# Mamba-style fusion kernel on one core: the second half of z goes through another PSUM bank and is copied to SBUF before its SiLU

## Chip, core and metric

The kernel runs on one core of a Trainium2 chip. The metric is the time of one execution on the device in microseconds (us). The version before the change takes 1730.51 us (median of three executions, 1729.14 to 1731.21).

## What is computed

64 sequences of 114 tokens (a class token, 36 image patches, 77 text tokens), width 256. After a layer norm comes a selective state-space block, then a gated feed-forward with a small mixture of experts. All is fp32. What matters here is the state-space block (D_INNER 512, 16 states):

```python
xz = x @ W_in
xi, z = jnp.split(xz, 2, axis=-1)
xc = silu(depthwise causal conv of xi, 4 taps, + conv_b)
dt, Bm, Cm = jnp.split(xc @ W_x, ...)
delta = softplus(dt @ W_dt + b_dt)
dA = exp(delta * A);  dBu = delta * Bm * xc
h = dA_t * h + dBu_t;  y_t = h . C_t          # scan over the tokens
y = ys + xc * D
return y * silu(z) @ W_out
```

## The kernel before

Sequences are taken two at a time: 32 groups of 2 x 114 = 228 columns. The code calls a group's turn a step `i`. Within step `i` the scan of group `i` is cut into 16 units `k`, each a [128 x 912] tile. For each unit:

- POOL (GpSimd) multiplies u by B into the SBUF ring `xr` (`dbu`, L1646);
- ACT (ScalarE) writes exp(delta * A) into one of two PSUM slots (`exps`, four instructions, L1010);
- DVE (VectorE) scans (L1307);
- the product with C is made by DVE (L1316) for ten units, and by POOL (L1654) for the six units listed in `ON_POOL`;
- PE (TensorE) adds the states up into bank YB (`reduce_states`, L711), with a D-term in front of every fourth unit (L708), which at units 0 and 8 waits until DVE has read the bank (`y_out`, L1324).

The other stages are hung on the units by hand, `if k == 7 and runs(i + 2)` and so on: the order on each engine is the order of these lines, and semaphores tie the engines together. Group `i+2` gets its tokens (L625 at k=0), centring (L635), variance (L642), x projection (L610) and convolution (L661). Group `i+1` gets B, C and dt (L685 at k=1), delta (L697), softplus (L1058 to L1066), and z (L610 at k=13). Groups `i-1`, `i-2`, `i-3` get the output projection, the second norm and the feed-forward: `ffn_in` L756, `ffn_sigmoid` L1102 to L1106, `v_center` L767 at k=0, its square L1110, `v_var` L771, `ln3_rstd` L1115 and L1117, `v_norm` L1390.

SiLU needs another activation table than exp and ln. So after the exps of unit 1 ACT has a "window": load the table, SiLU of x (four instructions, L1041), SiLU of z in two halves (L1047), load the first table back (L1132). The exps of unit 2 come behind it.

PSUM has eight banks: four for the two slots, YB, and AB, BB, CB, which all side stages share. Before the change z's first half is in AB, its second half in CB. CB also holds the convolution of x, so the second half of z cannot be projected before the window has taken x out of CB (`pe.wait_ge(xs_done, 2 * g + 3)` in `proj_z`). DVE's `y_out` at k=1 multiplies the last units' sum of the step before by silu(z).

The copy `dbl_copy` (L1052, ACT, ahead of the exps of unit 5) waits for L685. On ACT the exps of unit 5 and `ln3_rstd` stand behind it, and DVE's `v_norm` (after unit 4) waits for `ln3_rstd`; the scan of unit 5 stands behind `v_norm`.

Of the kernel before, what the change touches and what calls it, by code (L numbers as in the profile page):

```python
# [15 lines left out]
ON_POOL = (1, 3, 8, 10, 12, 14)  # L16


def fusion_kernel(nc, x_patches, txt_t, tok_w, tok_b, cls_t, pos_t, w_in, conv_w, conv_b, w_x, w_dt, b_dt,
# [42 lines left out]
    with ExitStack() as whole:  # L62
# [20 lines left out]
        with ExitStack() as ctx:  # L83
# [149 lines left out]
            def ffn_free(e, g):  # L233

                if g == GROUPS - 2:
                    e.wait_ge(var_mm, GROUPS)
                elif g == GROUPS - 1:
                    e.wait_ge(z_mm, 2 * GROUPS)
# [28 lines left out]
            def z_bank(half):  # L267
                return pair((AB, CB)[half])
# [76 lines left out]
            z_mm = sem("z_mm")  # L345
            sz_done = sem("sz_done")
            dbl_mm = sem("dbl_mm")
# [95 lines left out]
            with nc.Block() as block:  # L443
# [161 lines left out]
                def _(pe):  # L605
# [8 lines left out]
                    def bank_c(g):  # L614

                        need(pe, xs_done, 2 * g)
                        need(pe, sz_done, 2 * (g - 1))
# [27 lines left out]
                    def proj_x(g, p, half):  # L645
                        if half == 0:
                            pe.wait_ge(xh_done, g + 1)
                        elif runs(g - 4):

                            pe.wait_ge(x2t_ev, g - 3)  # L650
                        else:
                            need(pe, delta_done, 2 * g)
                        project(p, x_bank(half), 2 * half * P).then_inc(xi_mm, 1)
# [11 lines left out]
                    def proj_z(g, p, half):  # L665

                        if half == 1 and runs(g + 1):
                            pe.wait_ge(xs_done, 2 * g + 3)
                        elif half == 1:
                            pe.wait_ge(sz_done, 2 * g)  # L670

                        elif runs(g - 3):
                            pe.wait_ge(v_done, g - 2)
                        elif runs(g - 2):
                            pe.wait_ge(h2_ev, g - 1)
                        else:
                            pe.wait_ge(delta_done, 2 * g + 1)
                        project(p, z_bank(half), (CH + 2 * half) * P).then_inc(z_mm, 1)
# [9 lines left out]
                    def proj_delta(g):  # L688
                        pe.wait_ge(dbl_ev, g + 1)

                        if runs(g - 4):
                            pe.wait_ge(o_done, g - 3)
                        else:
                            need(pe, sz_done, 2 * g - 1)
                        for half in range(2):
                            for c in range(2):
                                mm = pe.matmul(dt_bank(half)[:, c], wdt[32:33 + R, (2 * half + c) * P:(2 * half + c + 1) * P],  # L697
                                               dbl[32:33 + R, :], start=True, stop=True)
                            mm.then_inc(dt_mm, 1)
# [34 lines left out]
                    def h2_turn(g):  # L734
                        pe.wait_ge(h2n_done, g + 1)

                        if runs(g + 3):
                            pe.wait_ge(delta_done, 2 * g + 8)
                        else:
                            pe.wait_ge(x2t_ev, g)  # L740
                        for k in range(DC):
                            for s in range(SEQ):
                                mm = pe.transpose(x2t_ps[:, k, s], h2n[0:T, s, k * P:(k + 1) * P], ident[0:T, 0:T])
                        mm.then_inc(x2t_mm, 1)
# [15 lines left out]
                    def v_center(g):  # L760

                        pe.wait_ge(v_done, g + 1)
                        if runs(g + 3):
                            pe.wait_ge(sz_done, 2 * g + 7)
                        elif g == GROUPS - 3:
                            pe.wait_ge(h2_ev, GROUPS)
# [19 lines left out]
                    def bias_rows():  # L786
# [3 lines left out]
                        pe.wait_ge(sz_done, 2 * GROUPS)  # L790
# [4 lines left out]
                    def before_first():  # L795
# [5 lines left out]
                        var(1)  # L801
                        for half in range(2):
# [3 lines left out]
                        for half in range(2):  # L806
                            proj_z(0, 0, half)
# [9 lines left out]
                    def body(i):  # L817
# [5 lines left out]
                        for k in range(UNITS):  # L823
# [26 lines left out]
                            if k == 13 and runs(i + 1):  # L850
                                proj_z(i + 1, 1 - p, 1)
# [6 lines left out]
                            if k == 7 and runs(i + 2):  # L858
# [135 lines left out]
                def _(act):  # L994
# [19 lines left out]
                    def center_out(g, p):  # L1014
                        act.wait_ge(cent_mm, g + 1)
                        need(act, z_mm, 2 * g - 2)
# [27 lines left out]
                    def z_silu(g, p, half):  # L1044
                        act.wait_ge(z_mm, 2 * g + 1 + half)
                        need(act, y_done, CH // 2 * (g - 2) + half + 1)
                        nc.scalar.activation(sz[:, p, 2 * half:2 * half + 2], z_bank(half), ACT.Silu).then_inc(sz_done, 1)  # L1047
# [76 lines left out]
                    def window(i, p):  # L1124
# [4 lines left out]
                        if runs(i):  # L1129
                            z_silu(i, p, 0)  # L1130
                            z_silu(i, p, 1)
# [4 lines left out]
                    def before_first():  # L1136
# [7 lines left out]
                        rstd_out(1)  # L1144
                        x_out(1, 0)
# [11 lines left out]
                    def body(i):  # L1157
# [5 lines left out]
                        for k in range(UNITS):  # L1163
# [20 lines left out]
                            if k == 12 and runs(i - 1):  # L1184
# [8 lines left out]
                            if k == 4 and runs(i + 1):  # L1193
                                dbl_copy(i + 1)
                            if k == 12 and runs(i + 2):
# [612 lines left out]
```

## Time and profile before

| | |
|---|---|
| median of three executions | 1730.51 us |
| the profiled execution | 1728.77 us, its span 1726.7 us |
| one step in the steady stretch (u at 727.66 and 776.92 us on POOL) | 49.26 us |
| granted clock of TensorE, mean of the span | 0.947 of full speed |

Busy time says how long an engine had an instruction running. Three engines are busy for nine tenths of the span, so the time is read from which of them waits for which in one step, and not from the busy shares. The steady stretch runs from some 200 us to 1540 us. Step 16 is the one that the rows show: its unit 0 is scanned from 800.41 us, its window on ACT runs from 800.61 to 806.44 us. PEclk in a row is the granted clock as a share of 2.4 GHz: 1.00 is 2.4 GHz, 0.50 is 1.2 GHz, values between are means of the two.

### The profile page before, as it was taken

The numbers are of one execution on the slowest core, as the hardware profiler recorded it, in microseconds if no ns is written. First come the engines' busy times: TensorE is split into PE (matmuls) and PEld (weight loads), VectorE is DVE, ScalarE is ACT, GpSimd is POOL, SyncE is SP. The second block draws the span as 40 slices with busy tenths as digits, with TensorE's granted clock in tenths as the row PEclk, the third lists the DMA queues.
The fourth block names the chain that finished last, engine by engine and source line by source line (L and its number), as shares of the span: only waits on it lengthen the run. The fifth ranks groups of instructions, "written<-read, shape, count | busy, mean of one in ns | idle before, by whom it ended". The sixth has DMA issues, their size and how long they took to land.

```text
span 1726.7 us, 28038 instructions
## 1 busy us (share of the span) xinstructions
PE 1480.7 (86%) x9868; PEld 1065.4 (62%) x9868; DVE 1555.7 (90%) x1389; ACT 1331.9 (77%) x3100; POOL 1564.6 (91%) x782
## 2 busy tenths in 40 slices
PE   7778898889888988898889889888889898977688
PEld 7555666666666666666666666666666666654355
DVE  2599999999999999999999999999999999999944
ACT  2577788888888888888888888888888888886644
POOL 0699999999999999999999999999999999999814
PEclk9888999999999999999999999999999999997899
DMA  4667755555656655656666555566665555656110
GB/s 141 138 135 180 163 130 123 122 131 132 145 129 146 132 123 122 131 130 146 129 146 135 122 125 126 130 146 129 145 138 121 125 126 129 142 119 141 36 34 15
DMA packets 194430, 218.47 MB, mean 127 GB/s; under 512 B 94011, under 2 KB 184773, under 8 KB 193778
## 3 DMA queue, kind: packets, MB, share of 16 engines
q1 hardware_dynamic: 193522, 215.51, 56.6%
q8 instruction: 78, 1.28, 0.3%
q0 software_dynamic: 576, 1.17, 0.3%
q14 instruction: 62, 0.51, 0.1%
q10 hardware_dynamic: 192, 0.01, 0.0%
HBM read 169.92 MB, written 47.09 MB: 126 GB/s over the span
## 4 chain that ended last, share of the span: by engine, by line
DVE 41%; ACT 18%; issue 16%; PE 13%; POOL 10%; DMA 2%; SPq 0%; DVEq 0%; ACTq 0%; POOLq 0%
DVE psum L1307 20%; DVE xr L1307 16%; ACT psum L1010 6%; POOL xr L1646 6%; POOL xr L1654 3%; PE psum L610 3%; DVE xr L1316 3%; ACT L1132 2%; PE psum L697 2%; PE psum L782 2%; ACT L1041 2%; ACT soft L1062 2%; ACT soft L1066 2%; ACT soft L1058 2%; PE psum L783 1%
## 5 line engine op out<-in xcount | busy, mean ns | idle before, releaser
L1646 POOL TENSOR_TENSOR xr<-u,bbc 128x912 f32<-128x912 f32 x512 | 1075.5, 2133 | 14.3 <-DMA u<-u_scratch 13.9
L1010 ACT ACTIVATE psum<-delta,a_neg 128x228 f32<-128x228 f32 x2048 | 805.9, 441 | 221.6 <-DVE xr L1316 191.2
L1307 DVE TENSOR_TENSOR_SCAN psum<-psum,xr 128x912 f32<-128x912 f32 x320 | 656.2, 2051 | 68.5 <-ACT psum L1010 59.8
L1654 POOL TENSOR_TENSOR xr<-xr,cbc 128x912 f32<-128x912 f32 x192 | 409.2, 2131 | 31.9 <-DVE xr L1307 28.5
L1307 DVE TENSOR_TENSOR_SCAN xr<-psum,xr 128x912 f32<-128x912 f32 x192 | 392.3, 2043 | 0.0
L1316 DVE TENSOR_TENSOR xr<-psum,cbc 128x912 f32<-128x912 f32 x320 | 353.7, 1105 | 11.1
L711 PE MATMUL psum<-xr,fold 128*32 128x228 f32 x4096 | 295.1, 385 | 50.6 <-POOL xr L1654 26.7
L610 PE MATMUL psum<-xh,win 128*128 128x228 f32 x1024 | 222.7, 367 | 61.8 <-ACT xs L1041 33.4
L610 PEld LDWEIGHTS psum<-xh,win 128*128 128x128 f32 x1024 | 192.1, 193 | 91.7 <-ACT xs L1041 44.0
L661 PE MATMUL psum<-xi,conv_d 128*128 128x228 f32 x1024 | 210.9, 358 | 0.0
L711 PEld LDWEIGHTS psum<-xr,fold 128*32 128x32 f32 x4096 | 96.9, 112 | 178.1 <-issue 79.4
L661 PEld LDWEIGHTS psum<-xi,conv_d 128*128 128x128 f32 x1024 | 190.2, 188 | 16.2 <-issue 11.7
L730 PE MATMUL psum<-wout,y 128*114 128x256 f32 x512 | 134.8, 411 | 0.0
L708 PE MATMUL psum<-xs,skip_w 128*128 128x228 f32 x256 | 83.2, 408 | 30.0 <-DVE y L1324 30.0
L730 PEld LDWEIGHTS psum<-wout,y 128*114 128x114 f32 x512 | 97.4, 200 | 18.8
L625 PE MATMUL psum<-xp,tokw 128*128 128x72 f32 x768 | 92.3, 278 | 8.4 <-DMA xp<-x_patches 8.4
L625 PEld LDWEIGHTS psum<-xp,tokw 128*128 128x128 f32 x768 | 92.8, 196 | 10.0 <-DMA xp<-x_patches 8.9
L1667 POOL TENSOR_TENSOR u<-delta,xs 128x912 f32<-128x912 f32 x31 | 65.9, 2125 | 18.4 <-issue 12.0
L708 PEld LDWEIGHTS psum<-xs,skip_w 128*128 128x128 f32 x256 | 40.9, 194 | 67.1 <-DVE y L1324 44.4
L697 PE MATMUL psum<-dbl,wdt 17*128 17x228 f32 x256 | 58.7, 369 | 22.2 <-ACT ob L1122 21.8
L697 PEld LDWEIGHTS psum<-dbl,wdt 17*128 17x128 f32 x256 | 46.0, 189 | 36.6 <-issue 34.0
L756 PE MATMUL psum<-x2t,w 128*128 128x228 f32 x256 | 58.8, 374 | 1.9
(204 smaller groups left out, 1574.7 us busy)
## 6 DMA issues: line engine op xcount, KB each, us to landing
delta<-delta_scratch SPq DMA_DIRECT2D x256, 228.0 KB, 6.5
u<-u_scratch SPq DMA_DIRECT2D x256, 228.0 KB, 4.2
bbc<-bc_scratch SPq DMA_DIRECT2D x128, 114.0 KB, 2.6
u_scratch<-u SPq DMA_DIRECT2D x64, 228.0 KB, 4.9
cbc<-bc_scratch SPq DMA_DIRECT2D x128, 114.0 KB, 2.7
delta_scratch<-delta SPq DMA_DIRECT2D x64, 226.0 KB, 5.7
out<-ob SPq DMA_DIRECT2D x32, 228.0 KB
h_scratch<-h SPq DMA_DIRECT2D x31, 228.0 KB
```

The lines of the kernel that those rows point to most:

```text
L610: mm = pe.matmul(bank[:, c], win[:, k, at + c * P:at + (c + 1) * P], xh[:, p, k], start=(k == 0), stop=(k == DC - 1))
L625: mm = pe.matmul(tok_ps[:, c, g % 2:g % 2 + count].rearrange("p h t -> p (h t)"), tokw[:, k, c * P:(c + 1) * P], xp[:, k, g % 2:g % 2 + co ...
L661: mm = pe.matmul(conv_bank(half)[:, c].rearrange("p (s t) -> p s t", s=SEQ), conv_d[:, at, t], xi[:, at, :, t:t + T], start=(t == 0), stop ...
L697: mm = pe.matmul(dt_bank(half)[:, c], wdt[32:33 + R, (2 * half + c) * P:(2 * half + c + 1) * P], dbl[32:33 + R, :], start=True, stop=True)
L708: pe.matmul(y_ps, skip_w[:, c], xs[:, i % 2, c], start=True, stop=False)
L711: mm = pe.matmul(y_ps[j * DQ:(j + 1) * DQ], fold[:], xr[:, k % XRING, j], start=False, stop=(n == NI - 1))
L730: mm = pe.matmul(h2_ps[:, s], y[:, g % 2, c, s * T:(s + 1) * T], wout[:, c], start=False, stop=(c == CH - 1))
L1010: ins = nc.scalar.activation(slot(k)[:, j * TOK:(j + 1) * TOK], delta4[:, c // 2, j, c % 2], ACT.Exp, scale=a_neg[:, c, j, n:n + 1])
L1307: nc.vector.tensor_tensor_scan(x if k in ON_POOL else slot(k), slot(k), x, 0.0, ALU.mult, ALU.add).then_inc(scan_done, 1)
L1316: nc.vector.tensor_tensor(xr[:, k % XRING], slot(k).rearrange("p (j t) -> p j t", j=J), cbc[:, p, k % NI].unsqueeze(1).to_broadcast([P, J, ...
L1646: nc.gpsimd.tensor_tensor(xr[:, k % XRING], u4[:, c // 2, :, c % 2], bbc[:, p, n].unsqueeze(1).to_broadcast([P, J, TOK]), ALU.mult).then_i ...
L1654: nc.gpsimd.tensor_tensor(xr[:, k % XRING], xr[:, k % XRING], cbc[:, p, k % NI].unsqueeze(1).to_broadcast([P, J, TOK]), ALU.mult).then_inc ...
```

## The change

The second half of z moves from CB to BB. Its projection moves on PE from k=13 to k=7, between the two halves of the x projection of the group behind; the second half of that x projection, which uses BB too, moves to k=8 and waits until z is out (`zc_ev`). A new ACT instruction `z_copy` at k=12 copies the raw half from BB to `sz` in SBUF; in the window the SiLU of this half reads and writes `sz`. Beside this `h2_copy` moves from k=12 to k=11, and the C product of unit 13 instead of unit 14 is POOL's. In `before_first` the second half of z of group 0 is projected ahead of x of group 1. The semaphore `z_mm` is split in two, and the waits are fitted.

```diff
-ON_POOL = (1, 3, 8, 10, 12, 14)
+ON_POOL = (1, 3, 8, 10, 12, 13)
...
             def z_bank(half):
-                return pair((AB, CB)[half])
+                return pair((AB, BB)[half])
...
                     def bank_c(g):
-                        need(pe, xs_done, 2 * g)
-                        need(pe, sz_done, 2 * (g - 1))
+                        need(pe, xs_done, 2 * g - 1)
...
                     def proj_x(g, p, half):
                         if half == 0:
                             pe.wait_ge(xh_done, g + 1)
-                        elif runs(g - 4):
-                            pe.wait_ge(x2t_ev, g - 3)
-                        else:
-                            need(pe, delta_done, 2 * g)
+                        elif g >= 1:
+                            pe.wait_ge(zc_ev, g)
...
                     def proj_z(g, p, half):
-                        if half == 1 and runs(g + 1):
-                            pe.wait_ge(xs_done, 2 * g + 3)
+                        if half == 1 and runs(g - 3):
+                            pe.wait_ge(x2t_ev, g - 2)
                         elif half == 1:
-                            pe.wait_ge(sz_done, 2 * g)
+                            pe.wait_ge(delta_done, 2 * g + 2)
...
                             if k == 13 and runs(i + 1):
                                 proj_z(i + 1, 1 - p, 0)
-                            if k == 13 and runs(i + 1):
-                                proj_z(i + 1, 1 - p, 1)
...
                             if k == 7 and runs(i + 2):
                                 proj_x(i + 2, p, 0)
...
-                            if k == 7 and runs(i + 2):
+                            if k == 7 and runs(i + 1):
+                                proj_z(i + 1, 1 - p, 1)
+                            if k == 8 and runs(i + 2):
                                 proj_x(i + 2, p, 1)
...
-                    def z_silu(g, p, half):
-                        act.wait_ge(z_mm, 2 * g + 1 + half)
-                        need(act, y_done, CH // 2 * (g - 2) + half + 1)
-                        nc.scalar.activation(sz[:, p, 2 * half:2 * half + 2], z_bank(half), ACT.Silu).then_inc(sz_done, 1)
+                    def z_copy(g, p):
+                        act.wait_ge(z_mm[1], g + 1)
+                        need(act, y_done, CH // 2 * (g - 1))
+                        nc.scalar.activation(sz[:, p, 2:], z_bank(1), ACT.Copy).then_inc(zc_ev, 1)
+
+                    def z_silu(g, p):
+                        act.wait_ge(z_mm[0], g + 1)
+                        need(act, y_done, CH // 2 * (g - 2) + 1)
+                        nc.scalar.activation(sz[:, p, 0:2], z_bank(0), ACT.Silu).then_inc(sz_done, 1)
+                        act.wait_ge(zc_ev, g + 1)
+                        nc.scalar.activation(sz[:, p, 2:], sz[:, p, 2:], ACT.Silu).then_inc(sz_b_done, 1)
...
-                            if k == 12 and runs(i - 1):
+                            if k == 11 and runs(i - 1):
                                 h2_copy(i - 1)
...
+                            if k == 12 and runs(i + 1):
+                                z_copy(i + 1, 1 - p)
                             if k == 12 and runs(i + 2):
                                 x_out(i + 2, 0)
```

On PE, from the convolution at k=12 of one step to L685 at k=1 of the next; `xh,win` is a projection (x8 both halves of z, x4 one), `xr,fold` the sum over a unit's states (x4 a unit). Before:

```order
L661 MATMUL psum<-xi,conv_d 128x228 x8
L711 MATMUL psum<-xr,fold 32x228 x4
L610 MATMUL psum<-xh,win 128x228 x8
L711 MATMUL psum<-xr,fold 32x228 x8
L708 MATMUL psum<-xs,skip_w 128x228
L711 MATMUL psum<-xr,fold 32x228 x4
L767 MATMUL psum<-vv,cent_h 128x228
L625 MATMUL psum<-xp,tokw 128x72 x12
L711 MATMUL psum<-xr,fold 32x228 x4
L685 MATMUL psum<-xs,wx 48x228 x4
```

The same place after the change:

```order
L661 MATMUL psum<-xi,conv_d 128x228 x8
L710 MATMUL psum<-xr,fold 32x228 x4
L613 MATMUL psum<-xh,win 128x228 x4
L710 MATMUL psum<-xr,fold 32x228 x8
L707 MATMUL psum<-xs,skip_w 128x228
L710 MATMUL psum<-xr,fold 32x228 x4
L767 MATMUL psum<-vv,cent_h 128x228
L627 MATMUL psum<-xp,tokw 128x72 x12
L710 MATMUL psum<-xr,fold 32x228 x4
L684 MATMUL psum<-xs,wx 48x228 x4
```

Four of the eight matmuls between the sums of unit 13 and of units 14 and 15 are gone; the rest keeps its order.

On PE, from the x projection at k=7 to the convolution at k=9. Before:

```order
L610 MATMUL psum<-xh,win 128x228 x8
L708 MATMUL psum<-xs,skip_w 128x228
L711 MATMUL psum<-xr,fold 32x228 x8
L756 MATMUL psum<-x2t,w 128x228 x4
L661 MATMUL psum<-xi,conv_d 128x228 x8
```

And after (the first x8 is half of x, then the half of z that moved):

```order
L613 MATMUL psum<-xh,win 128x228 x8
L707 MATMUL psum<-xs,skip_w 128x228
L710 MATMUL psum<-xr,fold 32x228 x4
L613 MATMUL psum<-xh,win 128x228 x4
L710 MATMUL psum<-xr,fold 32x228 x4
L756 MATMUL psum<-x2t,w 128x228 x4
L661 MATMUL psum<-xi,conv_d 128x228 x8
```

Four matmuls more stand ahead of `ffn_in` (L756) and of both convolutions.

On ACT, from the exps of units 10 to 12 to those of unit 14; `sz<-psum` is the new copy, `h<-psum` is `h2_copy`, `xi<-psum` takes x out. Before:

```order
L1010 ACTIVATE psum<-delta,a_neg 128x228 x12
L1076 ACTIVATE h<-psum 114x512
L1032 ACTIVATE xi<-psum 128x4x114
L1010 ACTIVATE psum<-delta,a_neg 128x228 x4
L1032 ACTIVATE xi<-psum 128x4x114
```

And after:

```order
L1010 ACTIVATE psum<-delta,a_neg 128x228 x8
L1084 ACTIVATE h<-psum 114x512
L1010 ACTIVATE psum<-delta,a_neg 128x228 x4
L1048 ACTIVATE sz<-psum 128x456
L1033 ACTIVATE xi<-psum 128x4x114
L1010 ACTIVATE psum<-delta,a_neg 128x228 x4
L1033 ACTIVATE xi<-psum 128x4x114
```

Between the exps of units 12 and 13 the copy of z takes the place of `h2_copy`, which now stands between those of 11 and 12.

## Rows read from the trace of the kernel before

**Rows 1.** The page, busy time of each engine, its share of the span, instructions
```profile
PE 1480.7 (86%) x9868; PEld 1065.4 (62%) x9868; DVE 1555.7 (90%) x1389; ACT 1331.9 (77%) x3100; POOL 1564.6 (91%) x782
```

**Rows 2.** Waits of DVE, 200 to 1600 us: total us, times, longest
```profile
DVE psum L1307 <- ACT psum L1010: 51.7, 29, 1.9
```

**Rows 3.** Timeline of POOL, step 15: start us, us, engine, line, [idle before]
```profile
779.84 2.12 POOL L1654 TENSOR_TENSOR xr<-xr,cbc 128x912 f32<-128x912 f32 x1 [0.80 <-DVE xr L1307]
```

**Rows 4.** Timeline of ACT, window of step 16 and what follows
```profile
804.59 0.55 ACT L1047 ACTIVATE sz<-psum 128x456 f32<-128x456 f32 x1 [0.77 <-PE psum L610]
...
808.14 0.36 ACT L1110 ACTIVATE vsq<-psum 128x228 f32<-128x228 f32 x1
...
811.31 1.58 ACT L1010 ACTIVATE psum<-delta,a_neg 128x228 f32<-128x228 f32 x4
812.96 0.35 ACT L1052 ACTIVATE dbl<-psum 48x228 f32<-48x228 f32 x1
...
815.25 0.36 ACT L1117 ACTIVATE psum<-vsq 128x228 f32<-128x228 f32 x1
```

**Rows 5.** Timeline of DVE, the same stretch
```profile
805.68 0.61 DVE L1324 TENSOR_TENSOR y<-psum,sz 128x456 f32<-128x456 f32 x1
808.07 2.07 DVE L1307 TENSOR_TENSOR_SCAN psum<-psum,xr 128x912 f32<-128x912 f32 x1 [1.78 <-ACT psum L1010]
...
813.35 2.06 DVE L1307 TENSOR_TENSOR_SCAN psum<-psum,xr 128x912 f32<-128x912 f32 x1
...
816.47 0.38 DVE L1390 TENSOR_TENSOR vv<-vv,psum 128x228 f32<-128x228 f32 x1
816.77 2.06 DVE L1307 TENSOR_TENSOR_SCAN psum<-psum,xr 128x912 f32<-128x912 f32 x1
```

**Rows 6.** Timeline of PE, the same stretch, granted clock 1.00
```profile
799.89 1.81 PE L610 MATMUL psum<-xh,win 128*128 128x228 f32 x8 [0.96 <-DVE vv L1385]
...
804.49 0.98 PE L711 MATMUL psum<-xr,fold 128*32 128x228 f32 x16
806.34 0.65 PE L708 MATMUL psum<-xs,skip_w 128*128 128x228 f32 x2 [0.88 <-DVE y L1324]
...
807.94 2.79 PE L625 MATMUL psum<-xp,tokw 128*128 128x72 f32 x24
...
811.18 1.74 PE L685 MATMUL psum<-xs,wx 128*48 128x228 f32 x8
```

**Rows 7.** Timeline of PE in steps 0, 14 and 15, all but the first row partly at low clock
```profile
58.46 0.59 PE L711 MATMUL psum<-xr,fold 128*32 128x228 f32 x8
67.48 5.39 PE L625 MATMUL psum<-xp,tokw 128*128 128x72 f32 x24 [8.43 <-DMA xp<-x_patches]
...
73.73 2.72 PE L685 MATMUL psum<-xs,wx 128*48 128x228 f32 x8
...
727.67 0.97 PE L743 MATMUL psum<-ident,h2n 114*128 114x114 f32 x4 [1.77 <-DVE delta L1357]
...
772.11 1.12 PE L708 MATMUL psum<-xs,skip_w 128*128 128x228 f32 x2
773.17 1.75 PE L711 MATMUL psum<-xr,fold 128*32 128x228 f32 x16
```

**Rows 8.** Stretches: PE, PEld, DVE, ACT, POOL busy (x instructions), PEclk, DMA, GB/s
```profile
60.00:64.00 4.00, 0.00 (x0) 0.00 (x0) 2.31 (x2) 3.11 (x9) 4.00 (x3) 0.76 1.06 222
...
72.00:76.00 4.00, 4.00 (x20) 2.21 (x20) 3.05 (x3) 0.00 (x0) 4.00 (x3) 0.53 0.24 55
...
727.00:731.00 4.00, 3.33 (x18) 2.22 (x19) 4.00 (x4) 2.80 (x9) 2.88 (x3) 0.59 0.61 116
```

**Rows 9.** Timeline of PE, both halves of the x projection of step 15
```profile
782.79 3.24 PE L610 MATMUL psum<-xh,win 128*128 128x228 f32 x16
```

**Rows 10.** Timeline of ACT, between the exps of units 12 and 13
```profile
787.25 0.53 ACT L1032 ACTIVATE xi<-psum 128x456 f32<-128x456 f32 x1
788.89 1.58 ACT L1010 ACTIVATE psum<-delta,a_neg 128x228 f32<-128x228 f32 x4 [1.11 <-DVE xr L1316]
```

More of the change, by code:

```diff
@@ L237, in ffn_free @@
                 elif g == GROUPS - 1:
-                    e.wait_ge(z_mm, 2 * GROUPS)
+                    for half in range(2):
+                        e.wait_ge(z_mm[half], GROUPS)
             def ffn_bank(g):
@@ L344, in fusion_kernel @@
             xs_done = sem("xs_done")
-            z_mm = sem("z_mm")
+            z_mm = [sem("z_mm%d" % half) for half in range(2)]
+            zc_ev = sem("zc_ev")
             sz_done = sem("sz_done")
+            sz_b_done = sem("sz_b_done")
             dbl_mm = sem("dbl_mm")
@@ L677, in proj_z @@
                             pe.wait_ge(delta_done, 2 * g + 1)
-                        project(p, z_bank(half), (CH + 2 * half) * P).then_inc(z_mm, 1)
+                        project(p, z_bank(half), (CH + 2 * half) * P).then_inc(z_mm[half], 1)
                     def proj_bcdt(g, p):
@@ L693, in proj_delta @@
                         else:
-                            need(pe, sz_done, 2 * g - 1)
+                            need(pe, sz_done, g)
                         for half in range(2):
@@ L739, in h2_turn @@
                         else:
+                            pe.wait_ge(zc_ev, GROUPS)
                             pe.wait_ge(x2t_ev, g)
@@ L763, in v_center @@
                         if runs(g + 3):
-                            pe.wait_ge(sz_done, 2 * g + 7)
+                            pe.wait_ge(sz_done, g + 4)
                         elif g == GROUPS - 3:
@@ L789, in bias_rows @@
                         pe.wait_ge(pool_c, 4)
-                        pe.wait_ge(sz_done, 2 * GROUPS)
+                        pe.wait_ge(xs_done, 2 * GROUPS)
                         for x in range(E):
@@ L801, in before_first @@
                         var(1)
+                        proj_z(0, 0, 1)
                         for half in range(2):
@@ L805, in before_first @@
                             convolve(1, half)
-                        for half in range(2):
-                            proj_z(0, 0, half)
+                        proj_z(0, 0, 0)
                     def after_last():
@@ L1015, in center_out @@
                         act.wait_ge(cent_mm, g + 1)
-                        need(act, z_mm, 2 * g - 2)
+                        for half in range(2):
+                            need(act, z_mm[half], g - 1)
                         nc.scalar.activation(xh[:, p], pair(CB), ACT.Copy).then_inc(cent_done, 1)
@@ L1129, in window @@
                         if runs(i):
-                            z_silu(i, p, 0)
-                            z_silu(i, p, 1)
+                            z_silu(i, p)
                         act.preload_act_table_set("natural_log_exp_and_others")
@@ L1144, in before_first @@
                         rstd_out(1)
+                        z_copy(0, 0)
                         x_out(1, 0)
```

## Prediction

> **What bounds the kernel now.** I read the page first: DVE, POOL and PE are each busy for about nine tenths [rows 1], so the shares don't say which one sets the time. Then DVE's waits: in the steady stretch it waits for one thing, the exps of unit 2, once a step, 51.7 us in 29 waits [rows 2]. The timeline of one step shows why. DVE runs out of work when `y_out` ends (805.68 + 0.61 = 806.29) and scans on at 808.07, 1.78 us later [rows 5], because ACT is in its window. There ACT itself waits 0.77 us for PE's second half of z [rows 4], which had to wait for the SiLU of x to leave bank CB. POOL has 0.80 us a step in which it waits for a scan [rows 3]. A step is 49.26 us, so DVE with its one hole, fed by ACT, sets the pace, and POOL would take over once 0.80 us were saved.
>
> Last I read PE and its clock, since the chain behind the window runs over PE: `y_out` releases L708 at 806.34, and L711, L767, L625, L711 and L685 follow without a gap up to 811.18 + 1.74 = 812.92 [rows 6]. `dbl_copy` starts at 812.96 right behind L685, the exps of unit 5 and `ln3_rstd` follow it up to 815.25 + 0.36 = 815.61 [rows 4], and `v_norm` could start then; it starts at 816.47, with the scan of unit 5 at 816.77 behind it [rows 5]. So this PE chain has 0.8 us of slack in a step, and no more.
>
> **Part by part, with TensorE's clock as it is.**
> - The window: `z_silu` loses its wait, 0.77 us. The SiLU from SBUF instead of PSUM has no row; its size is the one of 0.55 us [rows 4], I take it as equal, within 0.1 us. Exps of unit 2 and its scan come 0.77 us earlier, DVE's hole falls from 1.78 to about 1.0 us.
> - What is late next: the square L1110 at 808.14 [rows 4] needs L767, whose row would start at 807.45, behind L708 and L711, which start from `y_out` at 806.34 [rows 6]. `y_out` doesn't move against DVE's scans of units 0 and 1. So the square stays, and behind it the exps of unit 3, `h2_scale` and the exps of unit 4, 811.31 + 1.58 = 812.89. The scan of unit 4, now at 813.35 [rows 5], can come at 812.92: 0.43 us a step, not 0.77.
> - The copy: 0.53 us more on ACT (by `x_out`, same size), between the exps of units 12 and 13. These wait 1.11 us for DVE there before, and `x_out` ahead of them ends at 787.78 [rows 10]. `h2_copy` leaves this place and delays the exps of unit 12 by at most 0.2 us. The copy waits for its projection on PE, which comes 1.62 us (half of 3.24) behind the first half of x [rows 9]: 782.79 + 3.24 = 786.03, in time. Cost nothing; with the cover gone it would be what it is late.
> - The projection at k=7: 1.62 us more ahead of `ffn_in`, the convolutions and `proj_x` half 1, 1.62 us less behind unit 13. PE idles 0.96 us ahead of L610 at k=13 [rows 6], so it arrives there 0.7 us later than now.
> - Unit 13 on POOL instead of 14: the counts stay. POOL's product with C comes one product earlier, and PE's sum of unit 13 stands behind the convolution anyway. Nothing.
> - Start: group 0's projection ahead of group 1's costs PE 1.6 us, but step 0 waits for x_patches until 67.48 [rows 7]. Nothing. The end: the last window waits for z in both halves and may win some 1.5 us.
> That alone would be 29 x 0.43 + 1.5 = 14 us faster.
>
> **What the change does to PE's clock.** The moved projection was what kept PE at work beside ACT's window. Now PE reaches the half of z that is left at 799.89 + 0.7 = 800.6, does it in 1.8 us less the overlap, and sums units 14 and 15 (0.98 us) until 803.2 [rows 6]. Then it has nothing until `y_out` ends at 806.29: 3.1 us idle in a row, up to 3.9 us where waits inside the units 8 to 12 shrink. Before, the idle time there is in pieces, 0.96 us ahead of one half and 0.88 us behind the sums [rows 6], with the other half of z between. The rows show what such a hole does. In step 0 PE finishes at 58.46 + 0.59 = 59.05 [rows 7] and has nothing; and within 60 to 64, where it has no work at all, the clock goes from full to half (1.2 GHz), mean 0.76 [rows 8]. In the steady stretch it falls once a step after less than that: PE sums states, waits 1.77 us for delta [rows 7], and has 0.59 of its clock in the next 4 us [rows 8]. That fall costs little, the stages behind it have slack. This one would come just ahead of the chain with 0.8 us.
>
> The Trainium skill, page "TensorE: Matmul & The Clock Gate", section "HAM oscillation — how this bites in real kernels", says the same against this change: where PE waits in every tile, it falls back to half clock and starts each tile cold. The trace agrees in both places above; by a rule that only counts PE's work, which stays the same, the sum would be the 14 us gain.
>
> The chain at half clock, from rows at either level: L708 1.12 against 0.65, so +0.47; L767 has the same shape as L708, +0.47; each L711 1.75 against 0.98 for x16, +0.385 for x8, twice; L625 5.39 against 2.79, +2.60; L685 2.72 against 1.74, +0.98 [rows 6, 7]. Sum 5.3 us. It is not cut short by the work itself: in step 0 the clock stays at 0.5 through all of L625 and has a mean of 0.53 over 72 to 76 [rows 8], so it comes back only within L685. Less the slack of 0.8 us: 4.5 us a step if the clock falls before L708. If it falls only behind L767, the chain keeps 0.47 + 0.385 + 0.47: 3.2 us. I take 3.8, between the two. The 0.43 us is not won in such a step. `v_norm`, the output of group i-3, delta and its DMAs all shift with it; POOL and ACT wait.
>
> How often: the clock falls every step in a less empty place now. The chain with L625 exists in steps 1 to 29. I take 26 of these 29 steps: 26 x 3.8 = 98.8, less 3 x 0.43 and 1.5 at the end = 96 us. 1728.8 (profiled) + 96 = 1825; the median lies 1.7 us above the profiled execution, so I say **1826 us**. Ends: 16 steps at 3.2 and the rest at the gain give 51 - 6 - 1.5 = 44 us, 1774; 29 steps at 4.8 (with `v_var` cold too) give 139 us, 1869.
>
> **Rivals.**
> - *The clock holds through the hole* (faster). For it: the hole is bracketed by a projection and sums, and the idle pieces of 0.96 and 0.88 us before leave it at 1.00 [rows 6]. Against it: step 0, where 3 us of nothing were enough. It would give the 14 us: 1716; if the square were no limit, 0.77 a step, capped by POOL's 0.80, 24 us: 1707. It decides from one row: PEclk in the stretch behind `y_out`.
> - *The clock falls in few steps, or so late that only L625's end is cold.* 5 to 15 of 29 steps at 2 to 3.2 us, less the gain of the others: 1730 to 1773. For it: the fall in the steady stretch doesn't come at one fixed place of the step. Against it: 3.1 us is the longest hole of the step by far.
> - *The gain is given back on ACT* (no change). The copy comes when z is ready; if PE is 0.7 us later at k=7 than I think, the exps of unit 13 come late and DVE waits there for the 0.43 us it won: 1730. Against it: 1.11 us of waiting at that place [rows 10].
>
> **Chances.** Clock falls in most steps 0.74; in few 0.09; clock holds 0.13; given back 0.04. The likeliest case's own range is 1774 to 1869. The range for 8 in 10 reaches down over the few-steps case and leaves the faster one out: 1742 to 1862. About 0.2% (3.5 us) is what a measurement of this kernel can tell from no change. Faster 0.13, same 0.05, slower 0.82.
>
> **What would show it.** ACT's 0.77 us wait at the SiLU of z gone, DVE's hole ahead of scan 2 at about 1.0 us: the part meant is right. PEclk near 0.5 in the 6 to 10 us behind `y_out` of most steps, L625 at 5 us instead of 2.8, a new wait of 3 to 5 us on DVE near image tokens, `v_norm` or scan 5, the step at 52 to 53 us, POOL's idle up by 3 us or more a step: the forecast. If PEclk is 1.00 there and the step is 48.8 us, it is wrong and the first rival right. If the hole on PE is under 2 us, my timing of PE is wrong.

## Result and profile after

| | before | after |
|---|---|---|
| time, median | 1729.83 us (4 runs, 1729.10 to 1731.21) | 1767.29 us (4 runs, 1763.55 to 1791.79) |
| profiled execution, its span | 1728.77 us, 1726.7 us | 1791.79 us, 1789.7 us |
| granted clock, mean of the span | 0.947 | 0.891 |

The ratio is 1.020 [1.018, 1.023], and the medians differ by 37 us; the forecast was 96 us slower. Here and in the table of experiments a ratio leaves out an execution that lies more than 1.5% above the fastest of its kernel (1791.79 here, 1794.76 in e4). The profiled execution of the changed kernel is this slowest one. Executions of this kernel hold different numbers of steps of the slow kind shown below: three profiled ones have 17, 15 and 12 (this one, e4, and e6, which differs by one side edit) in 1791.79, 1777.71 and 1758.09 us.

The page of the changed kernel, busy time of each engine and the clock in 40 slices, against [rows 1]:

```profile
PE 1573.5 (88%) x9868; PEld 1125.5 (63%) x9868; DVE 1562.6 (87%) x1389; ACT 1336.5 (75%) x3132; POOL 1563.0 (87%) x782
...
PEclk8878898988999898889998989989997788998799
```

DVE, ACT and POOL are busy for within 7 us of what they were, in a span longer by 63 us: all three wait more. PE has the same 9868 matmuls and 93 us more busy time, so they run at a lower clock. DVE's waits from 200 to 1600 us (total us, times, longest), which answer to [rows 2]:

```profile
DVE vv L1400 <- ACT psum L1125: 48.8, 15, 3.3
DVE psum L1317 <- ACT psum L1010: 29.4, 39, 1.2
DVE h L1339 <- PE psum L627: 15.5, 15, 1.1
```

The old wait for the exps of unit 2 has shrunk from 51.7 to 29.4 us. Two new ones stand at `v_norm` and at the image tokens, 3.3 and 1.1 us each and 15 times, so in about every second of the 29 steps. A step is 48.77 us or 53.0 to 54.7 us; four lie between, at 50.1 to 52.1 us. Steps are counted from here on as the code counts them, from 0; the step that the rows of the kernel before call 16 (scanned from 800.41 us) is 15 by this count, and those called 14 and 15 are 13 and 14.

The timeline of PE up to the idle stretch (the hole) of step 16, which is a short step (881.24 to 930.02 us by DVE's scans of unit 0), against [rows 6]:

```profile
865.13 3.24 PE L613 MATMUL psum<-xh,win 128*128 128x228 f32 x16
...
882.11 1.81 PE L613 MATMUL psum<-xh,win 128*128 128x228 f32 x8
883.84 0.98 PE L710 MATMUL psum<-xr,fold 128*32 128x228 f32 x16
887.18 0.65 PE L707 MATMUL psum<-xs,skip_w 128*128 128x228 f32 x2 [2.36 <-DVE y L1334]
```

The same for step 17, a long one (930.02 to 983.22 us):

```profile
912.41 3.24 PE L613 MATMUL psum<-xh,win 128*128 128x228 f32 x16
...
929.88 1.81 PE L613 MATMUL psum<-xh,win 128*128 128x228 f32 x8
931.62 0.98 PE L710 MATMUL psum<-xr,fold 128*32 128x228 f32 x16
935.95 0.65 PE L707 MATMUL psum<-xs,skip_w 128*128 128x228 f32 x2 [3.35 <-DVE y L1334]
936.53 0.62 PE L710 MATMUL psum<-xr,fold 128*32 128x228 f32 x8
937.08 1.13 PE L767 MATMUL psum<-vv,cent_h 128*128 128x228 f32 x2
938.00 5.23 PE L627 MATMUL psum<-xp,tokw 128*128 128x72 f32 x24
943.16 0.99 PE L710 MATMUL psum<-xr,fold 128*32 128x228 f32 x8
944.08 3.27 PE L684 MATMUL psum<-xs,wx 128*48 128x228 f32 x8
```

The hole ahead of L707 is 2.36 us in one step and 3.35 us in the next. Behind the long one the chain that the prediction added up runs at half speed: L767 1.13 us, the tokens 5.23, the sums 0.99, L684 3.27. The stretches behind the two holes (columns as in [rows 8], the seventh number is PEclk):

```profile
888.00:892.00 4.00, 4.00 (x42) 3.29 (x34) 3.92 (x3) 2.98 (x10) 4.00 (x3) 1.00 0.00 0
...
937.00:941.00 4.00, 4.00 (x21) 3.83 (x18) 3.90 (x3) 2.69 (x9) 4.00 (x3) 0.50 0.02 4
941.00:945.00 4.00, 4.00 (x22) 2.80 (x22) 2.88 (x3) 1.93 (x6) 4.00 (x3) 0.50 0.08 15
```

ACT in step 17, against [rows 4]:

```profile
932.86 0.57 ACT L1053 ACTIVATE sz<-psum 128x456 f32<-128x456 f32 x1
933.29 0.61 ACT L1055 ACTIVATE sz<-sz 128x456 f32<-128x456 f32 x1
...
938.24 0.36 ACT L1118 ACTIVATE vsq<-psum 128x228 f32<-128x228 f32 x1 [1.45 <-PE psum L767]
...
947.38 0.35 ACT L1060 ACTIVATE dbl<-psum 48x228 f32<-48x228 f32 x1 [4.45 <-PE psum L684]
...
949.61 0.36 ACT L1125 ACTIVATE psum<-vsq 128x228 f32<-128x228 f32 x1
```

And DVE, against [rows 5]:

```profile
936.82 2.06 DVE L1317 TENSOR_TENSOR_SCAN psum<-psum,xr 128x912 f32<-128x912 f32 x1 [0.93 <-ACT psum L1010]
...
943.27 0.31 DVE L1339 TENSOR_TENSOR h<-psum,pos 128x144 f32<-128x144 f32 x1 [1.11 <-PE psum L627]
...
950.01 0.39 DVE L1400 TENSOR_TENSOR vv<-vv,psum 128x228 f32<-128x228 f32 x1 [3.32 <-ACT psum L1125]
```

In the window the wait of 0.77 us is gone, SiLU from SBUF takes 0.61 us beside 0.57 from PSUM, and DVE's hole is 0.93 instead of 1.78 us. The Trainium skill, page "Perfetto Trace Analysis", section "Optimizing Scalar/DVE Operations", gives ScalarE some 93 ns of data-access overhead on SBUF and 51 ns on PSUM, by which the SiLU from SBUF would be, as an estimate, 0.04 us longer; the trace agrees, with 0.04 us here and 0.06 against the 0.55 of [rows 4]. Then `dbl_copy` waits 4.45 us for L684, and 3.32 of them arrive at `v_norm`.

### The profile page after: what moved, and what is told of

It reads as the page before. It is cut to its first block, busy times and chain, and to the rows that moved or that the text cites. A ratio compares the mean times of both kernels' runs of the same rounds, so it can differ in the third digit from the quotient of the medians.

```text
span 1789.7 us, 28070 instructions
## 1 busy us (share of the span) xinstructions
PE 1573.5 (88%) x9868; PEld 1125.5 (63%) x9868; DVE 1562.6 (87%) x1389; ACT 1336.5 (75%) x3132; POOL 1563.0 (87%) x782
## 4 chain that ended last, share of the span: by engine, by line
DVE 28%; PE 23%; POOL 19%; issue 15%; ACT 13%; DMA 1%; SPq 0%; DVEq 0%; POOLq 0%; ACTq 0%
DVE psum L1317 12%; POOL xr L1656 11%; DVE xr L1317 10%; POOL xr L1664 7%; PE psum L627 6%; ACT psum L1010 5%; PE psum L684 3%; PE psum L710 3%; PE psum L637 2%; ACT soft L1070 2%; ACT soft L1074 2%; ACT soft L1066 2%; DVE xr L1326 2%; DVE y L1334 2%; PE psum L696 1%
## 5 line engine op out<-in xcount | busy, mean ns | idle before, releaser
L710 PE MATMUL psum<-xr,fold 128*32 128x228 f32 x4096 | 309.9, 395 | 36.3 <-DVE xr L1326 20.5
L707 PE MATMUL psum<-xs,skip_w 128*128 128x228 f32 x256 | 86.9, 423 | 83.9 <-DVE y L1334 83.9
L627 PEld LDWEIGHTS psum<-xp,tokw 128*128 128x128 f32 x768 | 138.0, 276 | 12.3 <-DMA xp<-x_patches 10.0
L627 PE MATMUL psum<-xp,tokw 128*128 128x72 f32 x768 | 136.6, 360 | 9.6 <-DMA xp<-x_patches 9.6
L729 PE MATMUL psum<-wout,y 128*114 128x256 f32 x512 | 142.0, 428 | 0.0
L707 PEld LDWEIGHTS psum<-xs,skip_w 128*128 128x128 f32 x256 | 43.0, 202 | 120.7 <-DVE y L1334 97.8
L729 PEld LDWEIGHTS psum<-wout,y 128*114 128x114 f32 x512 | 101.7, 208 | 20.8
L684 PE MATMUL psum<-xs,wx 128*48 128x228 f32 x256 | 83.2, 490 | 1.0 <-ACT xs L1042 1.0
L1060 ACT ACTIVATE dbl<-psum 48x228 f32<-48x228 f32 x32 | 11.3, 354 | 86.7 <-PE psum L684 85.3
```

The lines of the kernel that those rows point to most:

```text
L627: mm = pe.matmul(tok_ps[:, c, g % 2:g % 2 + count].rearrange("p h t -> p (h t)"), tokw[:, k, c * P:(c + 1) * P], xp[:, k, g % 2:g % 2 + co ...
L684: mm = pe.matmul(dbl_ps, wx[:, c], xs[:, p, c], start=(c == 0), stop=(c == CH - 1))
L707: pe.matmul(y_ps, skip_w[:, c], xs[:, i % 2, c], start=True, stop=False)
L710: mm = pe.matmul(y_ps[j * DQ:(j + 1) * DQ], fold[:], xr[:, k % XRING, j], start=False, stop=(n == NI - 1))
L729: mm = pe.matmul(h2_ps[:, s], y[:, g % 2, c, s * T:(s + 1) * T], wout[:, c], start=False, stop=(c == CH - 1))
```

## Experiments

There were two theories at the start. **A**: the time comes from TensorE's clock, which falls in the hole ahead of `y_out` and makes the chain behind it late. **B**: it comes from the new order of the side stages or from the copy, and the clock is beside the point. In what follows the hole is PE's idle time ahead of the D-term that waits for `y_out` (L707 or L708, by the kernel's line numbers), and a step is called cold when the granted clock is at half for more than 5 of the 10 us behind `y_out`. The counts are over steps 1 to 29 of each profiled execution. Ratios are to the kernel before, timed beside each. The median of the changed kernel was 1767.29 us in the first measurement and 1783.73 in e4, which was timed beside e1, e2 and e3; so how far another run lies from the changed kernel is known to some 16 us.

| run | us | ratio | hole, us | cold steps |
|---|---|---|---|---|
| e4, changed kernel again | 1783.73 | 1.029 [1.025, 1.033] | 1.96 to 3.36 | 15 |
| e6, unit 14 on POOL again | 1767.26 | 1.025 [1.022, 1.028] | 1.92 to 3.36 | 12 |
| e5, side edits alone | 1729.59 | 1.000 [0.999, 1.001] | 0.76 to 0.88 | 0 |
| e3, before without z's second half | 1838.08 | 1.063 [1.062, 1.064] | 2.99 to 3.77 | 27 |
| e8, e3 with 8 matmuls in the hole | 1732.16 | 1.002 [1.001, 1.003] | 1.54 in 27 steps | 5 |
| e7, changed with 3 | 1757.67 | 1.017 [1.015, 1.018] | 1.02 to 2.49 | 12 |
| e10, changed with 5 | 1751.61 | 1.013 [1.011, 1.014] | 0.55 to 2.04 | 10 |
| e1, changed with 8 | 1709.70 | 0.989 [0.987, 0.990] | up to 1.38 | 0 |
| e2, changed with tokens in the hole | 1713.28 | 0.991 [0.989, 0.992] | up to 0.53 | 0 |
| e12, changed, middle of the step busy | 1838.23 | 1.064 [1.062, 1.066] | 3.0 to 3.55 in 21 | 26 |
| e13, e12 with 8 in the hole | 1712.81 | 0.990 [0.988, 0.991] | up to 1.38 | 0 |
| e9, e1 with the square later | 1700.22 | 0.983 [0.981, 0.984] | up to 1.38 | 0 |
| e11, e2 with the square later | 1701.17 | 0.983 [0.982, 0.984] | up to 0.53 | 0 |

### The hole: e4, e1, e2

**e4** is the changed kernel as it is.

> The changed kernel itself, run again. Theory A (PE's clock falls in the hole that the moved projection leaves behind unit 15's sums, and the chain L707 to L684 then runs late): steps of two kinds only, 48.8 us where the granted clock stays at 1.00 behind y_out and 53 to 54.7 us where it falls; the time is 1712 us plus some 4.4 us for each step of the second kind, so 1760 to 1795 by their number. Theory B (the slowdown comes of the work that was added or moved: the copy on ACT, the projection at k=7, units 13 and 14): all steps are longer alike, also those at full clock.

1783.73 us, six executions from 1765.55 to 1794.76. The lengths of the steps are again 48.77 or 53.0 to 54.7 us, with three of 50.1 to 52.1, and the hole is 2.6 us or more in 14 steps, all cold. The Trainium skill says on the page "TensorE: Matmul & The Clock Gate", section "What's actually happening", that the number of matmuls that run at low clock at the start of a kernel varies from run to run. Here the like is seen in the middle of a kernel, with 17 cold steps in the first profile and 15 in this one.

**e1** puts matmuls without a use into the hole, in a bank that is free there:

```diff
+                            if k == 15 and 0 <= i and runs(i + 2):
+                                pe.wait_ge(xs_done, 2 * i + 5)
+                                for _ in range(8):
+                                    pe.matmul(psum[:, CB, 0:P], mean_w[:], mean_w[:], start=True, stop=True)
```

> The changed kernel with eight matmuls (128x128, result unused, into bank CB once x is out of it) between unit 15's sums and L707, on PE alone. Theory A: the clock no longer falls there, every step is 48.8 us, time 1710 to 1718 us, faster than both kernels, though PE does more. Theory B: nothing changes or it gets worse by some us, 1760 to 1800 us. If PE's extra work delays L707 by 0.5 us a step: 1725 to 1730.

1709.70 us, a little under A's range. PE in a steady step of e1:

```profile
893.96 0.98 PE L710 MATMUL psum<-xr,fold 128*32 128x228 f32 x16
894.86 2.05 PE L865 MATMUL psum<-mean_w 128*128 128x128 f32 x16
897.15 0.65 PE L707 MATMUL psum<-xs,skip_w 128*128 128x228 f32 x2 [0.23 <-DVE y L1338]
...
898.74 2.79 PE L627 MATMUL psum<-xp,tokw 128*128 128x72 f32 x24
```

With 2.05 us of work in the hole the tokens take 2.79 us in every step, and each of steps 3 to 29 is 48.76 to 48.78 us. The trace has 480 matmuls more (240 in the program, two in the trace for each), and the kernel is 74 us faster than e4, timed beside it, and 58 faster than the 1767.29 us of the first measurement. B has no account of this: the copy, the moved projection and both side edits are still there.

**e2** fills the hole with work that is needed: the tokens of group `i+3` at the end of unit 15 of step `i`, instead of those of group `i+2` at unit 0.

```diff
-                            if k == 0 and runs(i + 2):
+                            if k == 0 and i == 0:
                                 tokens(i + 2, 1)
...
+                            if k == 15 and 0 <= i and runs(i + 3):
+                                tokens(i + 3, 1)
```

> The changed kernel with the token projection (L625 before) taken from k=0 to the end of k=15 of the step before, so that real work stands in the hole and the chain behind y_out loses 2.7 us. Theory A: clock at 1.00 there, L684 done 2.7 us earlier, steps of 48.8 us or a little less (the square of v still waits for y_out), 1705 to 1716 us. Theory B: 1755 us or more.

1713.28 us, no cold step. Every third step is some 49.2 instead of 48.77 us.

### The kernel before with a hole: e3, e8

**e3** takes nothing from the change. It opens the hole in the kernel before by leaving out the projection of the second half of z, so that half of silu(z) is not what the reference has:

```diff
-                        project(p, z_bank(half), (CH + 2 * half) * P).then_inc(z_mm, 1)
+                        project(p, z_bank(half), (CH + 2 * half) * P).then_inc(z_mm, 2)
...
-                            if k == 13 and runs(i + 1):
-                                proj_z(i + 1, 1 - p, 1)
```

> The kernel before with the second half of z left out on PE (its SiLU reads what is in the bank; that half of z is not computed), so that it has the hole (3.7 us) but nothing of what the change adds. Theory A: though it does less work it is slower than before: the clock falls behind unit 15's sums in 15 to 29 of 29 steps at some 4 us, 1770 to 1830 us. Theory B: it is faster than before by the wait of 0.77 us that ACT loses, 0.4 to 0.8 us a step, 1706 to 1717 us.

1838.08 us, with 27 cold steps: less work and 108 us slower, 8 us more than A allowed. **e8** closes most of this hole again with e1's eight matmuls. The SiLU of the missing half reads `sz` in SBUF, so that the bank is free.

> The kernel before without the projection of the second half of z (as in the run at 1838 us; that half of z is left out, its SiLU reads SBUF), with 8 matmuls without a use behind the sums of units 14 and 15. It differs from the run at 1838 us by work that is added. Theory A: the clock stays at 1.00 behind y_out, every step is 48.7 to 48.9 us, 1705 to 1715 us, over 120 us faster with more instructions. Rival C (without z the order of PE's other stages against ACT and DVE is what costs the 3 to 5 us a step): the matmuls add 2 us of PE a step and nothing else, 1838 us or more.

1732.16 us, 106 us faster than e3 by added work. C, the rival of the expectation, is refuted, and A's number missed by 17 us: the hole is 1.54 us in 27 of the 29 steps, and 5 of those are cold. The hole ahead of L708 in e3:

```profile
911.42 1.13 PE L708 MATMUL psum<-xs,skip_w 128*128 128x228 f32 x2 [3.74 <-DVE y L1321]
```

And in e8, a warm step and the next, a cold one:

```profile
955.80 0.65 PE L708 MATMUL psum<-xs,skip_w 128*128 128x228 f32 x2 [1.54 <-DVE y L1327]
...
1004.58 0.65 PE L708 MATMUL psum<-xs,skip_w 128*128 128x228 f32 x2 [1.54 <-DVE y L1327]
...
1006.17 5.15 PE L625 MATMUL psum<-xp,tokw 128*128 128x72 f32 x24
```

Holes of one length, with the same work around them, end differently. So the length makes a fall likely and does not decide it alone.

### The size of the filling: e7, e10

e1 with `range(3)` and `range(5)` in place of `range(8)`.

> The changed kernel with 3 instead of 8 matmuls without a use in the hole behind the sums of units 14 and 15, some 0.8 us of work in it, so that the idle time of 2.4 to 3.4 us becomes 1.6 to 2.6 us. Theory A with the length of the idle time as what decides: most of the 15 or so cold steps go, few stay: 1708 to 1730 us, with 0 to 5 steps over 52 us. If only a hole that is nearly full keeps the clock up, the time stays at 1745 to 1780 us. Theory B: 8 fillers helped for another reason than the clock, 3 give a proportional part of it: about 1745 us, with every step 1 us longer than 48.77 us instead of a mixture of two lengths.

> The changed kernel with 5 matmuls without a use in the hole. With 3 (idle 1.35 or 1.74 us in front of L707) 11 to 13 steps stayed cold and the time was 1758 us, with 8 (idle 0.2 us) none and 1710 us. If the idle time decides with a sharp point between, 5 (1.3 us of work, idle about 0.9 to 1.2 us) is on the good side, since the kernel before had pieces of 0.96 and 0.88 us and no fall there: 1708 to 1714 us. If it goes in proportion to the work put in, 1727 to 1745 us with some 6 to 9 cold steps.

1757.67 and 1751.61 us. Both expectations of a sharp gain missed. For e7 the other branch holds (1745 to 1780 us, if only a nearly full hole helps); e10 lies outside both of its ranges. Against the 1767 us three matmuls take off 10 us, five 16 and eight 58. In e7 none of the 17 steps with a hole of up to 1.50 us is cold and all 12 with a longer one, from 1.59 us on, are. In e10 it is none of 16 up to 1.4 us and 10 of 13 at 2.04 us, such as this one:

```profile
869.52 0.65 PE L707 MATMUL psum<-xs,skip_w 128*128 128x228 f32 x2 [2.04 <-DVE y L1338]
870.11 0.70 PE L710 MATMUL psum<-xr,fold 128*32 128x228 f32 x8
870.74 1.13 PE L767 MATMUL psum<-vv,cent_h 128*128 128x228 f32 x2
871.66 5.24 PE L627 MATMUL psum<-xp,tokw 128*128 128x72 f32 x24
```

A filling that leaves part of the hole buys little.

### The side edits: e5, e6

**e5** is the kernel before with `ON_POOL` (..., 13) and `h2_copy` at k=11. **e6** is the changed kernel with `ON_POOL` (..., 14).

> The kernel before with only two of the side edits: the C product of unit 13 instead of 14 on POOL, and h2_copy at k=11. The second half of z stays in CB and is projected at k=13, so the stretch of PE beside the window is full. Theory A (the time comes from the clock that falls in the hole behind the sums of units 14 and 15): no hole, no new fall, 1726 to 1734 us, the same as before within 0.2%. Theory B (the changed kernel is slower because side stages moved, whatever the clock does): part of the loss shows here, 1740 us or more.

> The changed kernel with the C product of unit 14 on POOL again instead of 13. The prediction costed this edit at nothing. If so, the same mixture of steps of 48.8 and 53 to 54.7 us, 1762 to 1796 us. If unit 13 on POOL is what opens the hole (the sums of unit 14 would come later with it on POOL, and part the idle time in two), under 1740 us.

1729.59 us and 1767.26 us. The two side edits cost nothing and open no hole, as the prediction said. The copy and the moved projection are not in e5; that they cost nothing by themselves is what e1 and e2 show.

### Why only every second step: e12, e13

In the first profile of the changed kernel the hole is 2.6 to 3.4 us in 15 of the 29 steps, and all 15 are cold. In the other 14 it is 1.96 to 2.4 us, and 2 are cold and 2 partly. What makes it short shows in the middle of the step ahead, where PE waits for delta (L743) and the clock falls too. Two stretches of the changed kernel, in step 15 and in step 16 (PEclk 0.64 and 0.72):

```profile
859.00:863.00 4.00, 4.00 (x21) 2.86 (x14) 4.00 (x4) 3.92 (x11) 3.21 (x3) 0.64 1.13 182
...
904.00:908.00 4.00, 3.45 (x25) 1.47 (x24) 4.00 (x4) 2.83 (x7) 3.98 (x3) 0.72 0.08 22
```

PE in step 15, ahead of the short hole at 887.18:

```profile
857.77 0.58 PE L743 MATMUL psum<-ident,h2n 114*128 114x114 f32 x4 [1.77 <-DVE delta L1367]
858.69 0.99 PE L710 MATMUL psum<-xr,fold 128*32 128x228 f32 x8 [0.34 <-DVE xr L1326]
859.61 1.20 PE L726 MATMUL psum<-ident,h 128*114 128x128 f32 x4
860.60 2.52 PE L729 MATMUL psum<-wout,y 128*114 128x256 f32 x8
```

And in step 16, ahead of the long one at 935.95:

```profile
903.52 1.89 PE L644 MATMUL psum<-sq,mean_w 128*128 128x228 f32 x4
905.34 0.99 PE L710 MATMUL psum<-xr,fold 128*32 128x228 f32 x8
906.54 0.58 PE L743 MATMUL psum<-ident,h2n 114*128 114x114 f32 x4 [0.21 <-DVE delta L1367]
...
907.99 0.69 PE L726 MATMUL psum<-ident,h 128*114 128x128 f32 x4
908.52 1.89 PE L729 MATMUL psum<-wout,y 128*114 128x256 f32 x8
```

In step 16 the low clock comes ahead of the wait for delta, which absorbs it (0.21 us of waiting instead of 1.77). In step 15 it comes behind the wait, slows L726 and L729, and nothing takes that up until unit 13. So the projection at k=13 of step 15 starts 0.87 us behind DVE's scan of the next unit 0 (882.11, 881.24), and that of step 16 0.14 us ahead of it (929.88, 930.02). That is the 1.0 us by which the holes differ. All ten steps that are warm throughout stand behind a step whose fall in the middle came 20 to 27 us behind its `y_out`, so behind the wait. A cold step often is one of these, since its stages are late. This is feedback, theory **F**: a fall in the middle that comes late makes the next hole short, and so a cold step often protects the next one. It does so behind 9 of the 17 cold steps, two of these in part; steps 24 to 28 are cold in a row.

**e12** is to take the fall in the middle away. The variance matmuls move behind the sums of unit 6 and are done three times, with the same result.

```diff
-                        for k in range(DC):
-                            mm = pe.matmul(var_ps, mean_w[:], sq[:, k], start=(k == 0), stop=(k == DC - 1))
+                        for _ in range(3):
+                            for k in range(DC):
+                                mm = pe.matmul(var_ps, mean_w[:], sq[:, k], start=(k == 0), stop=(k == DC - 1))
...
-                            if k == 5 and runs(i + 2):
+                            if k == 6 and runs(i + 2):
                                 var(i + 2)
```

> The changed kernel with the variance matmuls (L644) moved behind the sums of unit 6 and done three times over (the same result), so that PE has 2 us more work just ahead of its wait for delta in the middle of the step, where its clock falls otherwise. Theory F (feedback: the fall in the middle makes PE late, which shortens the hole ahead of y_out to 2.2 us in every second step, and these steps stay warm): without the fall in the middle the hole is about 3.3 us in nearly every step, 24 to 29 of the 29 steps are over 52 us, the time is 1810 to 1840 us, which is the forecast's 1826: added work makes the kernel slower by 40 us or more. Rival G (the count follows from the sum of PE's work: more work, fewer falls): 1730 to 1765 us, fewer than 15 cold steps. Rival H (the place of the hole on the chip's own time decides, not its length): no change, 1762 to 1796 us.

> e12 with 8 matmuls without a use in the hole as well. It shows what the repeated variance matmuls cost by themselves: if nothing (PE has slack behind them), every step is 48.8 us and the time that of e1, 1707 to 1713 us. Were it 1720 us or more, part of e12's time would be this work and not the clock.

e12 takes 1838.23 us, 26 cold steps; e13 1712.81 us, none. PE in one step of e12, first its hole, then the place where the wait for delta was, and the stretch around that place:

```profile
1017.41 0.65 PE L708 MATMUL psum<-xs,skip_w 128*128 128x228 f32 x2 [2.90 <-DVE y L1335]
...
1038.45 2.58 PE L645 MATMUL psum<-sq,mean_w 128*128 128x228 f32 x12
1041.01 0.58 PE L744 MATMUL psum<-ident,h2n 114*128 114x114 f32 x4
```

```profile
1039.00:1043.00 4.00, 3.66 (x28) 2.75 (x27) 4.00 (x4) 3.21 (x8) 2.01 (x1) 1.00 0.22 59
```

The clock is at 1.00 in the middle here, against 0.72 in 904 to 908 us of the changed kernel, and PE doesn't wait for delta in steps 2 to 29. The fall is gone in 19 of the 29 steps. The other ten still have one, 17 to 20 us behind `y_out`, and behind eight of them the hole is one of the shorter ones (1.96 to 3.12 us; the one of 1.96 is warm). Over all, the hole is 2.9 us or more in 27 of the 29 steps. The added matmuls cost 3 us by themselves (e13 against e1), and where the hole is open the kernel is 71 us slower than the 1767.29 of the first measurement, 54 slower than e4. So the middle of the step sets the number of cold steps, as F says. G, which expected fewer, and H, by which the place in time alone decides, are refuted; that the place in time has a part is not.

### The gain that is there: e9, e11

The prediction cut the window's gain from 0.77 to 0.43 us because the square on ACT waits for L767. **e9** moves it, on top of e1, and **e11** on top of e2:

```diff
-                            if k == 2 and runs(i - 3):
+                            if k == 3 and runs(i - 3):
                                 v_square(i - 3)
```

> e1 (1709.7 us) with the square of the centred v (vsq, behind L767) moved on ACT from behind the exps of unit 2 to behind the exps of unit 3, so that these don't wait 0.96 us for PE. If the prediction's account of the 0.43 us is right (the gain of 0.77 us in the window is cut by this square), DVE's wait of 0.27 us ahead of the scan of unit 4 goes, a step is 48.5 us, the time 1701 to 1704 us. If POOL caps the gain first (it had 0.80 us of waiting, 0.49 are used), the gain stops at 48.46 us a step, which is about the same. If something else holds the scan of unit 4, 1710 us again. Risk: the square is 1.3 us later, v_var and ln3_rstd have slack for that (v_norm starts 0.4 us after ln3_rstd); if they don't, scan 5 waits and the time is 1710 us or more.

> The changed kernel with real work in the hole (the tokens of group i+3 at the end of unit 15, 1713.3 us alone) and the square on ACT behind the exps of unit 3, which gave 9.5 us beside the 8 fillers. Both waits ahead of the scan of unit 4 (0.27 us, and 0.61 us in every third step) should go: a step of 48.40 us, 1699 to 1703 us, level with the best run so far without work that has no use. If the 0.61 us came from another place than the square, every third step stays at 48.8 us: 1703 to 1706 us.

1700.22 us, 1 us under its range, and 1701.17, inside. ACT in e1 with its wait at the square, and in e11:

```profile
896.41 1.58 ACT L1014 ACTIVATE psum<-delta,a_neg 128x228 f32<-128x228 f32 x4
898.94 0.36 ACT L1122 ACTIVATE vsq<-psum 128x228 f32<-128x228 f32 x1 [0.96 <-PE psum L767]
```

```profile
892.21 3.08 ACT L1012 ACTIVATE psum<-delta,a_neg 128x228 f32<-128x228 f32 x8
895.23 0.34 ACT L1120 ACTIVATE vsq<-psum 128x228 f32<-128x228 f32 x1
```

The wait is gone, a step is 48.40 us, and both are 1.7% faster than the kernel before. e11 does it without a matmul that has no use.

## Why the prediction was right in direction and wrong in size

- **The window.** Forecast 48.83 us for a warm step (49.26 less 0.43), measured 48.77. What is late next was the square, as said: 0.27 us of DVE's wait stayed in such steps, and e9 removed it. The rival in which the clock holds (1716 us) would have come out at 1710: e1 shows the warm kernel, 20 us faster than before. Of this 27 x 0.49 = 13.2 us are steps 3 to 29; the rest lies in steps 1, 2 and 30 and at the end.
- **Side edits and copy at nothing.** Right (e5, e6, e1). From 200 to 1600 us the second half of x waits up to 0.40 us on PE for the copy in 9 steps, and the copy up to 1.0 us on ACT for its projection in 18; the exps of unit 13 behind it still wait for DVE (0.33 and 1.14 us in steps 15 and 16).
- **The hole opens and the clock falls behind it.** Right (e1, e2, e3, e8). Forecast 3.1 to 3.9 us idle, measured 1.96 to 3.36: the long ones fit, the short ones were not foreseen.
- **The chain at half clock.** Right: L767 1.13, tokens 5.23, sums 0.99, L684 3.27 us; the last was forecast at 2.72, because the clock does not come back within it in step 17. The price was 3.8 us over a step of 49.26, so 4.2 over a warm one; the 17 cold steps of the profile average 4.6 over 48.77.
- **How often: this is the step that failed.** "I take 26 of these 29 steps" was 17 in the profiled execution, 15 in that of e4 and, as an estimate, some 12.5 in the median one (1767.3 less the 1709.7 of e1, by 4.6). The argument was that the fall comes every step in a less empty place already. It took the hole as the same in every step, and read the fall in the middle from one step, behind the wait for delta, though one of its rivals says that the place varies. In the kernel before that fall is there in 27 of the 29 steps, in some ahead of the wait and in some behind it. In the changed kernel a fall behind the wait moves PE's later stages by 1 us and shortens the next hole to 2.2 us, and of the 14 steps with such a hole ten stay warm throughout. With the fall away in most steps (e12) the count is 26 and the time 1838 us. So the steps that the forecast had too many are those behind a late fall; that it is the length of their hole which keeps them warm is argued and not shown, see below.

The rest of the sum can be tested with the counts of the profiles in place of 26. For 17, 15 and 12 cold steps it gives 1787, 1778 and 1766 us, and the executions measured 1792, 1778 and 1758. It is sound to within 8 us, and in part because errors cancel: the price a little low for 17 cold steps (4.6 instead of 4.2 over a warm one), the gain outside the steady stretch too.

**What stays open.** Whether a hole of 1.5 to 2.5 us is cold. In the two profiles of the changed kernel and in e6, 3 of 43 steps with a hole of 2.0 to 2.5 us are cold; in e7 and e10, whose holes of that length stand behind the added matmuls, it is 16 of 19; in e8 5 of 27 at 1.54 us. So a hole of 2.2 us isn't safe by its length. No run separates what stands ahead of the hole from where it falls in time.

## What to carry to other kernels

When work is moved away from beside another engine's stage, look at what TensorE then has to do there, and fill the place with real work before counting the gain; here a cold step cost 4.6 us, and the removed wait gave 0.49. If an effect depends on a hole's length, ask what else changes that length from step to step: here a slow step often made the next one safe, and some half of the forecast events did not happen. Where a kernel's executions spread over 1.8% after a change (1763.55 to 1794.76 us) and over 0.3% before (1727.15 to 1732.40), look for steps of two lengths before averaging.

## What the runs showed of the hardware that was not expected

- Added matmuls made the kernel 58 us faster in one place (e1) and 71 us slower in another (e12), both against the 1767.29 of the changed kernel; against the 1783.73 of e4 it is 74 and 54 us.
- The half clock lasted through 8 us of uninterrupted matmuls: 937 to 945 us at 0.50, with PE busy for all of it.
- Leaving out a projection of 1.8 us a step made the kernel 6.3% slower (e3).
